# A two-layer sequence model on one core: the scan stage's preparation moved behind the first attention batch, and the order refitted

## The reference

```python
x = x + _L0_attn_ref(_layernorm(x), ...)   # "A": decayed linear attention, 16 heads of 8
x = x + _L0_ffn_ref(_layernorm(x), ...)    # "B": mixture of 8 experts, top 2, hidden 352
x = x + _L1_attn_ref(_layernorm(x), ...)   # "C": conv of 3 taps, silu, selective scan with 16 states, gate
x = x + _L1_ffn_ref(_layernorm(x), ...)    # "D": mixture of 8 experts, top 2, hidden 128, and 2 shared experts
```

## Time and profile before

| | us |
|---|---|
| median of 3 runs | 1718.2 |
| lowest and highest of them | 1715.0 and 7331.34 |
| the profiled execution | 1725.16 |
| its span, first to last instruction | 1723.4 |

### The profile page before, as it was taken

One profiled execution on the slowest core, in us unless ns is written; L12 is line 12 of the kernel. 1 busy time (PEld: TensorE's weight loads), 2 busy tenths in 40 slices (PEclk: granted clock), 3 DMA queues, 4 the chain that ended last, 5 costly groups with the idle time before them and its releaser, 6 DMA issues.

```text
span 1723.4 us, 29120 instructions
## 1 busy us (share of the span) xinstructions
PE 1375.9 (80%) x9192; PEld 927.2 (54%) x9192; DVE 1369.6 (79%) x2543; ACT 936.7 (54%) x1637; POOL 965.6 (56%) x571
## 2 busy tenths in 40 slices
PE   0778899999899985997989667978948875767688
PEld 0335377875567564675566434665614643534355
DVE  0689879798998895968999669489879588758846
ACT  0231354647765763567554675578456574585451
POOL 1000505288186493864867787740188677764776
PEclk9898899999999997999899669989979887888799
DMA  8620346676887585887778768899669788987953
GB/s 272 195 67 2 100 139 175 181 188 212 281 242 236 167 290 171 261 225 232 238 243 197 203 216 265 225 314 308 197 217 279 188 220 269 239 221 240 282 126 69
DMA packets 293905, 361.58 MB, mean 210 GB/s; under 512 B 33753, under 2 KB 234361, under 8 KB 293497
## 3 DMA queue, kind: packets, MB, share of 16 engines
q1 hardware_dynamic: 251512, 328.12, 61.2%
q0 software_dynamic: 42240, 31.61, 10.1%
HBM read 306.09 MB, written 55.50 MB: 210 GB/s over the span
## 4 chain that ended last, share of the span: by engine, by line
PE 30%; issue 20%; DVE 19%; POOL 10%; DMA 8%; ACT 7%; SPq 5%; POOLq 0%; DVEq 0%; ACTq 0%
POOL x L887 6%; PE bank L992 5%; DVE arena_c L1513 3%; PE bank L943 3%; PE bank L1064 3%; DVE arena_a L1440 3%; PE bank L952 3%; DMA arena_c<-bc_rows 3%; POOL rows L868 3%; DVE arena_c L1499 2%; DVE arena_c L1508 2%; PE bank L938 2%; DMA xg<-rows 2%; DVE arena_a L1451 2%; PE bank L910 2%
## 5 line engine op out<-in xcount | busy, mean ns | idle before, releaser
L887 POOL DMA_INDIRECT x<-outs,slot_idx x240 | 488.8, 2037 | 171.9 <-DMA outs<-yrow 88.3
L868 POOL DMA_INDIRECT rows<-xrow,slot_idx x240 | 356.9, 1487 | 85.8 <-issue 62.2
L992 PE MATMUL bank<-arena_c,ident 128*128 128x512 f32 x512 | 272.5, 663 | 34.9 <-DVE arena_c L1499 34.7
L1513 DVE TENSOR_TENSOR_SCAN arena_c<-arena_c 128x1024 f32<-128x1024 f32 x128 | 297.2, 2324 | 3.7 <-ACT arena_c L1271 3.3
L910 PE MATMUL bank<-xT_ring,mix 128*128 128x128 f16 (+1 forms) x1296 | 244.9, 227 | 59.6 <-DVE mix L1689 26.9
L912 PE MATMUL bank<-xT_ring,mix 128*128 128x128 f16 (+1 forms) x1296 | 244.3, 226 | 0.0
L911 PE MATMUL bank<-xT_ring,mix 128*128 128x128 f16 (+1 forms) x1296 | 244.2, 226 | 0.0
L1064 PE MATMUL bank<-mix 128*128 128x128 f32 (+1 forms) x1296 | 188.2, 291 | 40.9 <-ACT yrow L1316 19.7
L1064 PEld LDWEIGHTS bank<-mix 128*128 128x128 f32 (+1 forms) x1296 | 169.9, 201 | 74.8 <-issue 67.5
L910 PEld LDWEIGHTS bank<-xT_ring,mix 128*128 128x128 f16 (+1 forms) x1296 | 140.6, 108 | 106.0 <-issue 64.1
L1508 DVE TENSOR_TENSOR arena_c<-arena_c 128x1024 f32<-128x1024 f32 x128 | 160.4, 1256 | 26.6 <-DMA arena_c<-bc_rows 16.2
(11 more groups left out here) (223 smaller groups left out, 2366.1 us busy)
## 6 DMA issues: line engine op xcount, KB each, us to landing
arena_c<-bc_rows SPq DMA_DIRECT2D x256, 512.0 KB, 5.8
mix<-weights_B SPq DMA_DIRECT2D x168, 352.0 KB, 4.0
mix<-weights_B SPq DMA_DIRECT2D x168, 192.0 KB
xg<-rows SPq DMA_DIRECT2D x156, 129.0 KB, 4.2
outs<-yrow SPq DMA_DIRECT2D x156, 128.0 KB, 4.7
mix<-weights_D SPq DMA_DIRECT2D x144, 128.0 KB, 3.0
mix<-weights_D SPq DMA_DIRECT2D x144, 64.0 KB
rows<-mix SPq DMA_DIRECT2D x3, 2580.0 KB, 13.1
```

The lines of the kernel that those rows point to most:

```text
L868: pool.indirect_dma_start(out=xs_d[q % ROW_SETS], out_offset=bass.IndirectOffsetOnAxis(ap=slot_idx[:, q % RJ, c, j:j + 1], axis=0), in_=xr ...
L887: pool.indirect_dma_start(out=x[:, b, j, :], out_offset=None, in_=y_d[q], in_offset=bass.IndirectOffsetOnAxis(ap=slot_idx[:, q % RJ, c, i ...
L992: last = pe.matmul(bank[C_BANKS[h]][:], ident[:], half(hb[:, n % RR, :], h), start=(n == 0), stop=(n == NS - 1))
L1513: dve.tensor_tensor_scan(hb[:, n % RR, :], dA[:, n % RDA, :], hb[:, n % RR, :], 0.0, ALU.mult, ALU.add).then_inc(c_scan.sem, 1)
```

## The change

Only `ORDER` is different. Its first line, before and after:

```diff
-    "AACACAAAAAAAAAAAAAAAAWAAAAAAWWoAAsAoWAAosAAwqAwsWwokAPkqsowqwWsAwoqAqwsoqAswokAqsCoqsAoqsoAwskwowqAqWoAswswq"
+    "AAAAPAAAAAWAAAAAAAWAAAAAAAAWAoAAsAAkAoAWoAswqskAwWwoqsoAkwqskowqAwqsAwkokqsoqsAokwAqsAoqsAowsowwqqAWWosAswwq"
```

More of the change, by code:

```diff
@@ L120 @@
[L120 removed]
+    "AAAAPAAAAAWAAAAAAAWAAAAAAAAWAoAAsAAkAoAWoAswqskAwWwoqsoAkwqskowqAwqsAkwokqsoqsAokwAqsAoqsAowsowwqqAWWosAswwq"
+    "AwoAokwqsswoAqwqsqAWWwWAAAAAAAAAPAAAAAAAAAPAAAPkAkoAsAokAqAswwoAqPwPsoAAkAqwsoPqsoPPPWqPPACwCoCAwssoqsoqsoAw"
+    "AwkqqAossokqkwwwqossAAPqwwAoqwkPsoAPoAwwsqsqqAWPwwPWAAPAPAAPWAWAAAAAAAAAAXPAAAAXAAXoAAPsAosAoXkwqkAqkosPkoKA"
+    "kswwqqosAoAXXAPwPkPAsosqosqwwoseAPAwwqKPkoPqsqoPwseqPoAqwsXoqXswAwskRRTARUTUMqLwRMLwoMKqRVsVTUAwLoUUAqNeUPwK"
@@ new lines @@
+    "TASLwUsAZUqMRVLVNwATLVAUUTPMKALAAUMXeURZVVCVAPLPAPNUZUKLReeANATZPUMAAVAVRKPKPAAXUPPRUALVAXAAXASLAKULNAVAAUZo"
+    "UTAULsRXqNkoMAVsULZVkPLUTqPUAwoTSwMAsoVsMVLXkPUKUkALokqsSLqKUekwoSsqPAwoAVSTwVosqAUMeowUAUXKNqAwsLPskoqRPVwo"
+    "ASsseowkNqLVsPqAUUVwZoPqwLTAURqPwsZMoesSwqAVNULoqsPZAAUoPLPPUwqKwTMXAALwwsAqSULVVwPRZVUAPKeNAeUPVALGRTNMUVPA"
+    "USKLPAUPTSeZKSPPMNAGPPZUPRGePVPPLGeUNAPLTRAAPAAMVARPUAZAKANAUPLAASZUUVPLTVXARVGAGAoNAMTUUUeeLAGLVVZNMAoLUSks"
+    "LoGUZsksMqkKASoLqUsZwoAMNkTwqUVTALVKsUeUAoLUXVqRVoskkwXATURqoswsALKVKULNqoUVkMALCwTqoCUMsRsCewkqUoAVswwoCqCq"
@@ new lines @@
+    "AXVUCqCALwCXCCCUCoCXKAZLCeCRCsCUoCSCsCAXSLsSCKCXCCXCCNwoACXAwXVwwZqbTCseASqNUoMVXUZqbqwsCLUdwqdwAVwNAAxZTARh"
+    "AMAdAcAAASAAwXbUxXchLAAPKeXpAAbLxpAAVAhxAAcPPdUNSVpALAAUybohZxdosehXVPdAxycboNKApTdkRZNSBeMhcUTspRGbAUyPULyM"
+    "RKqoVqUecbSsGcwLxwpLPkeyPTUGRkKZsRVPbhMocUAVpVxqhPLdKPAPNUTNZPoxVMUGyLsUPPAdUbyLqcdPVTULphMUoSxVSshVLKwAUqZe"
+    "qNRTkwUbUoxLNwTZsVAUcUdwUpRVqodkesMKKbALyhARoeMLsZVkoNLeGwqkSGwsUcVKUwRAqbpTcbkMLwyxZTsLAUdoSVUpLdNoqAVdUeyh"
+    "qMZKswUASyRbsNoSLxURULZsxAUVeTwVochqToKqSRsLVwMpVqAApeNwMsdyUwTUqUKNUwVwLqUVchpeUbZGKNVLAMxSLZwPyyPhAcZPUAVA"
@@ new lines @@
+    "GLeAxAAeATUPpRMyLAPUVPSLAUAPTVPUKMLRPAhpUTMcVNLPPZRyAPUCCKPCPUVCAUeCCACXLPNUVUTARXLPCCXVCCMXPCCKACPLCPCCACXC"
+    "CCUXAKLCSPZCACCVCCXARCCPAoPXeAKXoACXTAsCSMNSCVcUsCoAACUNZVLscVLqUUqLAbXXUbekoZexwSxXdRdPsqNPZPPSohVkUxTbXAbd"
+    "NAMopuuVhTvLZxNspTlwhqKRdSsyUSXeMyUkevxRcUdblKZpbwVkLLoVUMwhcqXcAqdpnkbGGUhLeKxGnoUKkpsahLybSyckbAySdNxVUosc"
+    "VpoRdwZcqLhAUSUNesPRAxwVRxTkyoZqLUqVKwpTMUTbdUebVLKwssePUMNAVwLcUhSNPURVKopZSPVMhLLqbydAxosZxUpdhcPcNLKRPwbo"
+    "MTLPUypUAdPAVqeydUsLMwVUwUoSLqxTyPGcBAhVZUwVpeLsNTRUUhVqyuZxVhvpwxuLlTbKMleGNqowdcZvyNRMsGpUdZUKdASqyncheLnL"
@@ new lines @@
+    "bsVMSUUapVwyLRTxqwhRUcpUNbKAxLScVyVUhZUTVepALUMNLyVCAUCSCKGACRewZeCSUGUKLVRATLNCMRCTUZVAACUKANPLURCAeMZCVTSU"
+    "UKCLReMNLCVCZSPPUALCUVTUUPLVGMTVVCMGCCLUPCKCGAUPLUPTCKVCPMPURCSPPKPPCCLePVCGUPXLPCeCNCSPUVCCCAPNCKCPRbZUVTLN"
+    "ZeUVcCXVLRMbLdUAUNAxhAxUZAdZAPdXALKpAhUxAbRATcpeAAAXAMVSbcUoULVPAehXoPTsyxXXdMVLNUhLqXcdAyKXVdUdpobSyLUsxNkb"
+    "AZSXPupXZSkXXxVNsoXUvPueleNhAVhLqSxSbkvZZsonccpylhnpbxKuSRdvdhclybxulPywaPRTvwAdUqhPnXUMdpPPbLPeLxMosbnVpPUh"
+    "sPacTcKdSKXwypkUPeckAUAbVLKxBURZNokcqRLMyqPVTsbywwkUpcRhAToxpVKqhRGdGeNxsLUwSVoVGKTpsUeTqNcMZRMAbVLGyhGqSpeN"
@@ new lines @@
+    "wyLToZdbKAqNKMcwkRMsZUZMxoRwThRqSyxVLpcdMAbehGUxdeTwKywyKcVoGhNGpUpGLKGNUZTssSZoeMeCKVAsLeSyqyAqeRCKZCTCRoNV"
+    "wCeCUMLqLUVSwMNsAoCKeqTwUZRLMsTNRLACGwKSqKZGwoCeUCSVCRSsCKTwCqMwLCPeDSCCPNTCCZMCRCUVPCeCKPKCCCeSKeVGGCULPCPe"
+    "VCPPCCVRLPCNPGPGNPPZCPcCRGbTcPKMSNCbPPZSUZZTdNMRPxNdLRUVSPhTbxeSUTVTLBSMGNUMGRdbdLxeVKNGchRKXcUbXSSZLpTSNhpy"
+    "VcPpeZdbUcbNZTMMSxXyVNLdZXXhXUPpXeXXVcZXcMbXxxLLPPdhbXVPPPpubXSbhbZXylXpxXhpxdPyyxycxdGydNychpxvhPKuhndppbvP"
+    "ZhyxpScucGydnvRRuTxlyPhncabldUnpbdcvhTGlxpRGUGxVyMLUdTLhMRabUPLpcRdVZyhcUMGyKxUphNpVyMCTyRCSCVCUCULeeCUKKLSN"
@@ new lines @@
+    "LVZTMVRUeUTNULCCCCVCCUCKLCMVPCUZLCUGCeGGLCCCRCVCTVKZeRNGUCCNSCCCLGZCCCCUSUeUSTMRUCNLVCVCPKVUUMbbULZLPVeVNLTc"
+    "cUKTbSUxRdbxhdLVMPUGZLLUKUGedNKVcRPTbMdyxUbZVpNhpUPUPxhLRecMVPKVybxULNUZpyhcxLeTUPdePpUVcNSPbRVKhTdcVSxpUhpL"
+    "hMxVyLhbZPdcybpKdLUTMxpdVMUVLZyUyNUhSUdLxZyULcRLTVSpdedcMbyeuVhRpPNcbKxlhyTZPNuxnvcZUyPhbpUlvKxUUMPpLnPdbVhx"
+    "dcxpddPVLLhbVGyLTUUaVMyRUcNpULUKyechPLSbVuGKypRTVcxulMvKhUpyleRLNCCvZZCCCSUNUCZSBLMTGCSnVenVUTCNCCReCLUCGaCM"
+    "XUCPKVePCCCSCZLCGUeCCPCXSKVCPCCCNCCXVKLCCCCCXUXXUbCxVbLcPhXxydPpcbXydxhehbycdpPdpddZXNXyxSddShecbZXPxhcbcbPy"
@@ L121 @@
+    "VNuLSZVEENSTLSueNUZlEEvnvnKuTVZGeNuGlUMnaRZnEvFGFFSNLOlOvFFOKZFOSVOMFleESLOaJGFGSOGJGIFGSIIFGZEFISOIOIFIIIGI"
+    "OFOOFOIGGFIGIOGFGGIGIIGGOJQJJQQOJQQJQJJQJJQJQQJQQJQJQJQQQ"
 )
```

54 lines of the change are left out of this document (10 added, 44 removed).

## The result

| | before | after |
|---|---|---|
| median, runs taken side by side | 1720.1 us | 1700.2 us |
| ratio, 95% interval | | 0.988 (0.987 to 0.990) |
| the profiled execution | 1725.2 us | 1692.5 us |
| its span | 1723.4 us | 1690.8 us |

The changed kernel is 20 us faster, 1.2%; 1681 was forecast, with 1662 to 1703 as the range. The time lies in the range, 19 us above the forecast and outside the 1673 to 1690 that the forecast case gave itself. So the sum has to be judged by medians, and the traces by the places where the advance shrinks.

A forecast was written before the change was run, and what follows sets the result against it. Head waits for stage C's weights stalled three engines, with TensorE and VectorE about 80% busy: 1725.2 − 38 (head) + 1.0 (taps) + 0 (small moves) = 1688.2, less 7.0 from profiled execution to median = 1681 us, range 1662 to 1703.

The forecast's parts named there:

- the forecast case: Whole kernel: head's advance kept, small moves neutral, 1681 us, own range 1673 to 1690; chance 0.50.
- (a): Head, ScalarE: first normalisation can start at about 9.9 instead of 48.89, 39.0 us earlier.
- (b): Head, TensorE: `ready B` moved forward, first transpose waits for `Wg_0w` until 12.56 instead of 49.53, 36.9 us earlier.
- (c): Head, VectorE: three maxima of staged weights, 7.21 us, end at about 23.9, hidden before the first `a_outer` at 25.0.
- That it lasts: Head to end: no absolute time, such as the sync engine's load list, holds the rest; the 38 us carry through.
- The taps: VectorE, batch 1: three scalings of line 1466 leave the idle head and add 0.7 to 1.4 us, taken as 1.0.
- The small moves: Whole order: steps moved 6 places on average, put at 0 with 12 us to either side; job 3's stall stays.
- The port rule: Job 3's scatters: two-input VectorE and SBUF-reading GpSimd instructions exclude each other, so the 18.2 us stall stays.
- rival 2: One more of nine jobs exposes an 18.2 us stall like job 3's: 1699 us; chance 0.23.
- Rival 3: Small moves remove job 3's stall, or as much in small waits: 1663 us; chance 0.22.
- Rival 4: Slower than before: row loads wait behind scatters at several job starts, 18.2 us each, 1736 us; chance 0.03.
- the case that had 0.42: Whole kernel: the measured time within 2% of before, 34.4 us to either side; chance 0.42.

The follow-up runs named there:

- m_head: The kernel before with only `ready C`, `conv_taps` and `conv_weights` put to places 198, 200 and 202: 1685.8 us, ratio 0.980.
- h_early: The changed kernel's order in the first 2,400 places, the remaining steps as `m_head` has them: 1688.7 us beside 1724.7 for the kernel before, 0.980.
- q_dve: The changed kernel with only VectorE's queue in the order of `m_head`: ratio 0.984 to the kernel before.
- r_refit: The changed kernel with `ready C`, `conv_taps` and `conv_weights` put back to places 2, 4 and 81: 1743.1 us, ratio 1.015 to the kernel before.
- after_again: The changed kernel unchanged, run once more beside the others on one chip: 1702.7 us, ratio 0.990 to the kernel before.
- fix_down: The changed kernel with two `c_sum` steps of batch 6 put behind batch 5's last `sh_down` on TensorE: 1698.4 us beside 1720.1 before, 0.990.

## Why the prediction was right and wrong

**The bound, and what the head's change removes: right.** (a) was 9.9 and is 10.24. (b) was 12.56 and is 12.04, because `Wg_0w` landed half a microsecond earlier. (c) was right on the maxima: due to end at 23.9, ended at 23.35, and `a_outer`, due at 25.0, started at 23.77. The gain at `a_outer` is 39.25, at the first store of line 719 38.3, and 39.7 at the first `slot_idx` and at the first load of line 734 (149.6); 38 was taken. The ring order that the Trainium skill states (DMA: Bandwidth & Descriptors, "Queues, rings and completion order") had spoken for `ready B` as the last to let TensorE go, and the trace agrees: the first transposes wait 12.04 us for this load. But as a term of the gain (b) was not the one that counted, since TensorE's start at 10.33 in `m_head` gave no earlier `a_outer`.

**That it lasts: right, with a smaller size in the medians.** In the profiles `m_head` is 38.3 to 46.0 us ahead of before from the first `shift_C` to the end. The medians say 34 and, for `h_early`, 36. The sum's terms, −38 + 1, are in between. The profiled execution of before lay 5 us above its median, and a gain taken between two single executions carries that with it. None of the absolute times bit: SP's list ended at 72.3 and the first store came at 74.12.

**The taps: not contradicted.** The three scalings stand at 100.6 to 101.0, where 102 was forecast, and TensorE's next value product waited 1.26 us instead of the 0.91 of the one ahead. One microsecond can't be told from the rest.

**The small moves at nothing: wrong, by 15 to 17 us on top of the moved head (23 alone), and this is nearly the whole miss.** The step that failed reads "The order printed in the change shows the same rows ahead of that load as before, and the load is the same number of steps from its user. So this stall stays, and I put the small moves at 0, with 12 us to either side." It compared SP's and GpSimd's queues around the load. Both were indeed alike, and the stall did stay. But its length is that of the scatters, and theirs depends on VectorE's sequence beside them, which was not compared: one scatter went from 8.96 to 15.94 us, and the stretch around it grew by 7.1. The other part is a spread of waits in batches 2 to 7 of the scan; the ones that were tried are not worth their own length, and the cause of the rest stays open. The 12 us were also too narrow: the 18.2 is a row, but that the small waits come to two thirds of it had none.

**The port rule: read too coarsely.** From the rule that the Trainium skill states on the shared port pair (SBUF — State Buffer) the prediction concluded that "the same work lies beside the same scatters after the change". The same work in another order was not the same cover: `q_dve`, which differs from the changed kernel in VectorE's order alone, has the 8.98 us.

**The rivals.** The time, 1700, is that of rival 2, 1699, but its mechanism is not what happened: no further stall of 18 us stands at any job's start, and job 3's waits 20.76 instead of 18.19. Rival 3 did not happen. Rival 4 was away from it by the head's gain alone, though its direction was the right one: `r_refit`, without the moved head, is slower than before. The chances 0.22 and 0.23 for the small moves to win or lose 18 us were symmetric; the runs put the moves on the side of rival 2, and no row that was read before told the side. The time lies in the range only because this had been widened to the times of rivals 2 and 3; in that there is luck. Faster by over 2% had a chance of 0.55 and did not come; the 1.2% is the case that had 0.42.

**By its own criteria** the text named the case: the starts right and the advance shrinking, to be seen where rows are less than 37 us early. That is first so at 380 (36.6), but there the advance comes back to 38.4 by 581; from 604 (35.3) and 745 (30.7) on it is so at most places, though not at 1365 (39.9).

The best orders measured are `m_head`, with only the three steps at the head moved, and `h_early`, both 0.980.

## What to carry to other kernels

When a wait for a load stops three engines at the head, the gain of moving it is that of a chain read forward from the landings, and here it was kept to the end, since the later work waits for semaphores and not for a time. Price it apart from whatever else is in the change: here three moved steps won 34 us, and the small moves of most of the other 4,914 gave half of it back. Where GpSimd issues scatters beside a saturated VectorE, compare VectorE's sequence too, and don't count a wait that a swap removes as won before the next load behind it has been looked at.

## What the runs showed that was not expected

The same kind of indirect scatter of GpSimd takes from 0.97 us up to 8.96 or 15.94 us beside a VectorE without a pause, and the longest of job 3's takes the same time to 0.02 us in every kernel whose VectorE sequence is the same there.

Removing a wait of 6.17 us between two engines brought 6.8 us of waits for row loads in the next 12 us. In the scan's part of the span the rows come at 239 to 245 GB/s with the DMA engines 82 to 86% busy. The windows of `after_again`:

```profile
974.00:1376.00 402.00, 307.88 (x2008) 200.11 (x2007) 317.62 (x512) 252.40 (x402) 233.46 (x139) 0.89 0.82 244
1376.00:1584.00 208.00, 136.31 (x706) 85.74 (x706) 155.19 (x207) 113.81 (x185) 126.27 (x84) 0.83 0.84 239
```

and of `m_head`:

```profile
970.00:1369.00 399.00, 312.35 (x2018) 202.01 (x2019) 319.25 (x513) 255.12 (x404) 236.47 (x141) 0.90 0.82 245
1369.00:1570.00 201.00, 132.80 (x703) 79.30 (x702) 154.09 (x208) 113.83 (x184) 135.21 (x82) 0.83 0.86 244
```

The same work takes 402 and 208 us instead of 399 and 201, with TensorE idle a third and VectorE a quarter of the second stretch. That the loads set part of the pace there would fit the waits for rows in `fix_down`; it was not tried.

The granted clock from 64 to 77 us is 1.00 (2.4 GHz) in the changed kernel, where it was 0.61 before, but the work of that stretch is another now. The same work stands 39.25 us earlier, from 24.75 to 37.75, and there the clock reads 0.57 (mostly 1.2 GHz), with TensorE 8.62 of 13 us busy as before. So the low clock came along with the work, and costing it at nothing was right here. The column does not show everything: the first matmuls of line 938 (with `cs_w`) last 1061 ns each, at 52.6 us before and at 14.0 now, where it reads 1.00. That is what these matmuls last where it reads 0.50 (1060 to 1063 ns at 176 to 182 us of the kernel before); where it reads 1.00 later, from 75 to 78 us of the changed kernel, they last 592 to 617.
